# Feed-forward in chunks of 256 slots, started in the same block as attention

## The reference: one transformer block with routed experts

```
q, k, v = x @ Wq + bq, x @ Wk + bk, x @ Wv + bv       # 16 heads of 8 features
for each window of 64 tokens (starts 0, 32, ..., 192) and head:
    ow += softmax(q_w k_w^T / sqrt(8) + pos_bias) v_w
merged = ow / (number of windows that hold the token)
x = layernorm(x + merged @ Wo + bo)
vals, idx = top_k(x @ router_w.T, 2)                  # 8 experts
g = sigmoid(vals); g = g / (g.sum() + 1e-10)
for each expert e:
    h = silu(x @ w_gate[e]) * (x @ w_up[e])           # 256 hidden
    out += g_e * (h @ w_down[e])
x = layernorm(x + out)
```

## Time and profile before

| | us |
|---|---|
| median of 3 runs | 1024.05 (1019.09 to 1028.25) |
| the profiled execution | 1033.48, its span 1031.6 |
| attention up to the last context product | about 665 of the span |
| last projection to first gate product | 666.3 to 706.8 |
| chunks | 706.8 to 981.2 |
| POOL's last result DMAs | 981.2 to 992.3 |
| final block | 992.3 to 1031.6 |

### The profile page before, as it was taken

How to read it: one execution, slowest core, us unless ns; L and a number is a source line. 1 busy time by engine, 2 the same in 40 slices (tenths; PEclk the granted TensorE clock), 3 DMA queues, 4 the chain that set the end, 5 groups by cost and what they waited for, 6 DMA issues and landing times. The chain is left out here.

```text
span 1031.6 us, 32316 instructions
## 1 busy us (share of the span) xinstructions
PE 777.2 (75%) x13248; PEld 588.0 (57%) x13248; DVE 501.3 (49%) x1592; ACT 323.0 (31%) x483; POOL 442.9 (43%) x502
## 2 busy tenths in 40 slices
PE   5789789798798797887887977716887888888700
PEld 2477566475575565654755655515776667767600
DVE  7446355363453453543545544444455544554537
ACT  3134323233233232332332322204333322332218
POOL 8312533524425425234244243260555555546555
PEclk9899898898898988988989989857989889888955
DMA  6973343243233332432433220033222222221157
GB/s 179 263 218 97 95 121 100 80 129 104 67 112 103 101 94 86 128 102 65 132 95 89 85 64 22 9 112 94 83 78 78 68 67 83 81 70 57 37 213 301
DMA packets 79858, 107.33 MB, mean 104 GB/s; under 512 B 15648, under 2 KB 59296, under 8 KB 79712
## 3 DMA queue, kind: packets, MB, share of 16 engines
q1 hardware_dynamic: 70048, 85.44, 27.6%
q0 software_dynamic: 9088, 18.76, 5.4%
q10 hardware_dynamic: 576, 1.07, 0.3%
HBM read 61.05 MB, written 43.71 MB: 102 GB/s over the span
## 5 line engine op out<-in xcount | busy, mean ns | idle before, releaser
L613 DVE TENSOR_REDUCE neg_max<-score_ps 128x16 f32<-128x1024 f32 x109 | 133.5, 1225 | 262.6 <-PE score_ps L891 172.7
L1094 POOL DMA_INDIRECT results<-scaled_sb,result_at x156 | 149.9, 961 | 142.7 <-DVE scaled_sb L1165 98.9
L258 POOL DMA_INDIRECT slots<-rows_sb,slot_at x128 | 125.5, 980 | 172.9 <-DVE slot_at L730 127.7
L565 ACT ACTIVATE prob<-scoret_ps 128x1024 f32<-128x1024 f32 x112 | 114.6, 1023 | 249.9 <-PE scoret_ps L891 167.4
L944 PE MATMUL o_ps<-v_sb,prob 128*32 128x18 f32 x7168 | 108.4, 190 | 74.2 <-issue 74.2
L944 PEld LDWEIGHTS o_ps<-v_sb,prob 128*32 128x32 f32 x7168 | 88.2, 114 | 93.6 <-issue 86.9
L441 POOL TENSOR_TENSOR expo<-euler,neg_top 128x8 f32<-128x8 f32 x16 | 26.4, 1648 | 154.6 <-DVE neg_top L684 154.5
L1154 DVE TENSOR_TENSOR h_sb<-silu_sb,score_ps 128x512 f32<-128x512 f32 x39 | 26.7, 686 | 129.0 <-ACT silu_sb L1116 99.0
L928 PE MATMUL scoret_ps<-max_rows,half 128*64 128x512 bf16 x448 | 69.6, 390 | 19.2 <-DMA max_rows<-maxt_sb 15.6
L911 PE MATMUL scoret_ps<-bias_hl,fold 128*64 128x512 f16 x448 | 74.7, 416 | 0.9 <-ACT prob L565 0.4
L891 PE MATMUL scoret_ps<-blocks,stack 128*64 128x256 f16 x920 | 71.8, 278 | 0.0
(11 more groups left out here) (162 smaller groups left out, 1484.4 us busy)
## 6 DMA issues: line engine op xcount, KB each, us to landing
scratch<-qk_hl SPq DMA_DIRECT2D x128, 128.0 KB
stack<-scratch SPq DMA_DIRECT2D x32, 512.0 KB
blocks<-scratch SPq DMA_DIRECT2D x128, 128.0 KB
xin<-slots SPq DMA_DIRECT2D x39, 260.0 KB
final_y<-results SPq DMA_DIRECT2D x16, 512.0 KB, 6.9
x_sb<-in_x SPq DMA_DIRECT2D x16, 256.0 KB, 3.9
out<-y_sb SPq DMA_DIRECT2D x16, 256.0 KB, 4.7
slots<-fill SPq DMA_DIRECT2D x11, 260.0 KB
```

Source lines behind the costliest of these rows:

```text
L258: nc.gpsimd.indirect_dma_start(slots, bass.IndirectOffsetOnAxis(ap=slot_at[:, n:n + 1], axis=0), rows_sb[:, n // TT, n % TT, :], None).the ...
L565: act.activation(prob[:, (par + u) % 2, :], scoret_ps[:, :, :].rearrange("p b c -> p (b c)"), ACT.Exp).then_inc(exp_done, 1)
L613: dve.tensor_reduce(neg_max[:, par, v, :], ps[:, :, :].rearrange("p b (h k) -> p (b h) k", k=W), AX_X, ALU.max, negate=True).then_inc(max_ ...
L1094: pool.indirect_dma_start(results, bass.IndirectOffsetOnAxis(ap=result_at[s % RBUF][:, t:t + 1], axis=0), scaled_sb[:, s % RBUF, t, :], No ...
```

## The change

**Chunks.** 256 slots instead of 512, hence 71 instead of 39: 64 full and 7 spare. Each chunk has one `gate_up` of twelve matmuls of 256 slots, a `turn` of two transposes, a `down` of eight matmuls, and two indirect DMAs of 128 rows. Silu (L697) and `hidden` treat both halves of the hidden features in one instruction of 128x512.

**Weights.** Their high and low parts are made once per expert, in attention steps 4 to 11, one expert in each (`weights_high` on ACT, `weights_low` on DVE). Per chunk, ACT copies the two parts of its expert to one of three buffers (`weights_in`, L685, 128x1024).

**Table.** It is made in two pieces. The first 45 entries are made of chunks that are full after the 13th step; they are counted in step 14 (`count_known`) and written in the last step (`place_known_a`, `place_known_b`). The other 26 entries are made of pieces dealt out over chunks 13 to 21.

**No barrier.** The chunk loop stands in attention's block. `turn(0)` comes ahead of the last two contexts, `gate_up(0)` ahead of `project_out(15)`. What is left of step 15 is dealt out: PE projects after chunk 0, turns x1 after 5, makes logits after 7, ranks after 10; DVE does the residual in chunk 1, the norm in 4, and the rest in 7 to 22; POOL computes `powers(15)` after the results of chunk 4 and issues the 8 scatters of step 15 one at a time after the results of chunks 14, 16, ... 28. Spare rows are filled after load 8, expert rows after load 30. Load 45 waits for all scatters, fills and the second piece of the table.

**Scatters.** `scatter(13)` is split: four DMAs in step 14, four in the last step. `scatter(14)` runs in the last step, ahead of the first results.

**Memory.** The buffers of the chunks stand beside attention's instead of on top of them, some on `blocks` and `stack`, which are free by then.

```diff
-FULL = TOP * N_TOK // TOK
+HALF = 256
+HT = HALF // P
+FULL = TOP * N_TOK // HALF
+KNOWN = STEPS - 4
+FIRST = ((KNOWN + 1) * TOP * TOK - E * (HALF - 1) + HALF - 1) // HALF
+WBUF = 3
 # SP
+                for s in range(SLOT_CHUNKS):
+                    if s == FIRST:
+                        sp.wait_ge(filled, 16 * (SPARE + E))
+                        sp.wait_ge(scattered, 16 * TOP * TT * STEPS)
+                        sp.wait_ge(tables, 2)
+                    slots_in(s)
...
 # POOL, step and tail
+                    if last:
+                        scatter(i - 2, range(TT, TOP * TT))
+                        make_fill()
                     if not first:
                         powers(i - 1)
-                    if not first and not last:
+                    if i == STEPS - 3:
+                        table_constants()
+                    if i == STEPS - 2:
+                        scatter(i - 1, range(0, TT))
+                    elif not first:
                         scatter(i - 1)
...
-                scatter(STEPS - 2, range(0, 1))
                 deviation(STEPS - 1)
-                scatter(STEPS - 2, range(1, 4))
-                powers(STEPS - 1)
-                scatter(STEPS - 2, range(4, TOP * TT))
-                scatter(STEPS - 1)
+                for s in range(SLOT_CHUNKS):
+                    results_out(s)
+                    if s == 4:
+                        powers(STEPS - 1)
+                    if 14 <= s < 14 + 2 * TOP * TT and s % 2 == 0:
+                        scatter(STEPS - 1, range((s - 14) // 2, (s - 14) // 2 + 1))
 # ACT
+                def weights_in(s):
+                    e = table_value(act, expert_at, s, E - 1)
+                    after(act, up_ps, s + 1 - WBUF)
+                    settle(act)
+                    act.copy(w_slot[:, s % WBUF, :, :], wgu_sb[:, e, :, :]).then_inc(w_ready, 1)
...
+                for s in range(SLOT_CHUNKS):
+                    silu(s)
+                    if s + 2 < SLOT_CHUNKS:
+                        if s + 2 == FIRST:
+                            act.wait_ge(tables, 2)
+                        weights_in(s + 2)
+                        high(s + 2)
 # DVE
+                for s in range(SLOT_CHUNKS):
+                    hidden(s)
+                    if s >= LATE:
+                        scale(s - LATE)
+                    if s + 2 < SLOT_CHUNKS:
+                        low(s + 2)
 # PE
+                def gate_up(s):
+                    after(pe, h_done, s - 1)
+                    pe.wait_ge(x_low, s + 1)
+                    pe.wait_ge(w_ready, s + 1)
+                    b, w = s % HBUF, s % WBUF
+                    for n, signal in ((0, gate_ps), (1, up_ps)):
+                        for hh in range(2):
+                            cols = slice(n * HID + hh * P, n * HID + hh * P + P)
+                            out_ps = (score_ps, scoret_ps)[s % 2][:, n, hh * HALF:(hh + 1) * HALF]
+                            pe.matmul(out_ps, w_slot[:, w, 0, cols], x_lo[:, b, :], start=True, stop=False)
+                            pe.matmul(out_ps, w_slot[:, w, 1, cols], x_hi[:, b, :], start=False, stop=False)
+                            last = pe.matmul(out_ps, w_slot[:, w, 0, cols], x_hi[:, b, :], start=False, stop=True)
+                        last.then_inc(signal, 1)
...
+                for s in range(SLOT_CHUNKS):
+                    if s == FIRST:
+                        pe.wait_ge(tables, 2)
+                    e_before, e_of = e_of, table_value(pe, expert_at, s, E - 1)
+                    gate_up(s)
+                    if s == 0:
+                        project_out(STEPS - 1)
+                    if s == 5:
+                        turn_x1(STEPS - 1, 1)
...
+                    if s + 2 < SLOT_CHUNKS:
+                        turn(s + 2)
+                    if s:
+                        down(s - 1, e_before)
+                down(SLOT_CHUNKS - 1, e_of)
```

More of the change, by code:

```diff
@@ new lines, in build @@
+        qk_free = qk_f[:, :, :].rearrange("p n t -> p (n t)")
+        hl_free = qk_hl[:, :, :, :].rearrange("p n h t -> p (n h t)").bitcast(F32)
+        xt_free = xt_sb[:, 0, :]
+        region, marks, upto, number = (reuse(qk_free, early, *n) for n in ((E,), (E, PARTS), (E, E), (FIRST, E)))
+        taken, full, cum, jump, ahead, rem, rise = (reuse(qk_free, early, E) for _ in range(7))
+        first_of = reuse(qk_free, early, E + 1)
+        over, at_most, summed = (reuse(hl_free, wide, *n) for n in ((E, PARTS), (E, E), (E, E)))
@@ L748, in step, with weights_low @@
                             top_two(i - 1)
[L749 removed]
+                        if u == (6 if last else 8) and not first:
                             places(i - 1, 1 - par)
[L752 to L761 removed]
+                def weights_low(e):
+                    dve.wait_ge(w_high, e + 1)
+                    settle(dve)
+                    dve.tensor_tensor(wgu_sb[:, e, 1, :], wgu_sb[:, e, 1, :], wgu_sb[:, e, 0, :],
+                                      ALU.subtract).then_inc(w_low, 1)
                 done = [0]
@@ L804, in _ @@
+                for s in range(SLOT_CHUNKS - LATE, SLOT_CHUNKS):
+                    scale(s)
             @block.tensor
@@ L1005, in step @@
                                 bias_s(i + 2, 0)
+                        if u == NU and last:
+                            turn(0)
                         if u >= 2:
```

545 lines of the change are left out of this document (290 added, 255 removed).

## The result

The changed kernel takes **988.25 us** (median of 4 runs, 983.22 to 991.23), the kernel before 1025.09 (4 runs). The ratio is 0.964 with a 95% interval of 0.958 to 0.971. I had forecast 980, in a range of 904 to 1046. The profiled execution took 986.44, its span 984.7; my sum was 987.7 for the span.

What follows compares the result with a forecast made beforehand. The prediction took POOL's indirect DMA runs holding up PE's results to bound the chunk stage. Terms -39.8 + 7 - 17.5 + 10.4 - 4 = -43.9 gave span 987.7; plus 1.9 minus 9.4 gave 980 us, range 904 to 1046.

Steps and rivals of the forecast that it cites:

- hold: In attention and chunks: a few us into a gapless run of POOL's indirect DMAs, PE's results reach no engine until it ends.
- final block: The program's last stage, 39.3 us in the profile before: forecast unchanged, 0.
- Handover: From attention to the chunks: first gate product at 667.0 instead of 706.8, -39.8 us; bounds -41 and +3 later.
- Chunks: Chunk loop: 3.61 us per chunk of 256, times 71 = 256.3 against 273.8, so -17.5 us.
- scatter(14)'s +7: Last attention units or first chunks: its eight DMAs, now run together, cost 8.95 less 2, +7 us; bounds 0 and +9.
- The charge of 0.51 us per indirect DMA: Chunk stage: cost of the hold per POOL indirect DMA, (7.02 - 4.99) / 4; charged twice per chunk of 256.
- Step 15 inside the chunks: Chunk loop: PE 3.3, POOL 4.1 for eight more indirect DMAs, DVE 3; sum +10.4 us, bounds +4 and +16.
- End: POOL's queued results after the last chunk: 7 us instead of 11.1 before the final block, -4 us; bounds -8 and 0.
- No hold: Rival, chunks and scatters: gaps break POOL's runs, chunks take 2.59 us and the +7 goes; 897 us, chance 0.2.
- Short runs: Rival, chunk loop: runs of four DMAs with pauses of 4.24 us, 4.5 us per chunk; 1043 us, chance 0.18.
- Exposed loads: Rival, gate products: each 256-column product pays one more weight load of 0.106 us, 90 us in all; 1070 us, chance 0.05.
- It does not do what it says: Rival, handover: a queue wait keeps the first chunks back until step 15 is through, 25 of 40 us return; 1005, chance 0.1.

## Why the prediction was right, and where it was not

The times of both chips beside the terms, changed minus before, from the traces, with all four stages cut at the same events in both kernels:

| Term | forecast | first chip | chip without hold |
|---|---|---|---|
| first gate product | -39.8 | -40.4 | -40.8 |
| chunks with scatter(14) and step 15, up to the last `scale` | -17.5 + 7 + 10.4 = -0.1 | 270.47 - 274.53 = -4.1 | 197.45 - 195.52 = +1.9 |
| from there to the first load of the final block | -4 | 7.8 - 11.0 = -3.2 | 10.1 - 17.2 = -7.1 |
| final block | 0 | 40.1 - 39.3 = +0.8 | 40.2 - 39.2 = +1.0 |
| span | -43.9 | -46.9 | -45.0 |

- **Handover: right,** to 0.6 us. Nothing that `turn(0)`, the table or the weights need was late. One thing shown beside it was off: I expected PE's clock back from the 0.5 of the handover, and the first chunk's products are still 0.21 us apart, which costs about 1 us. This row is most of the change in the span, but not all of it is gain, since part of the work that stood there is paid inside the chunks. On the chips without hold the parts can be told apart by kernels, each against the kernel before on its own chip: chunks of 256 without early start are 16.7 us faster, with the early table 38.7, with step 15 dealt out 47.2. So the early start is worth some 30 of the 47 there; on the first chip these kernels did not run.
- **Chunks: right in mechanism, wrong by 4 us.** The mean of 3.75 us lies inside the 3.3 to 4.0 that I had named. It holds step 15 in it; less the 10.4 that I had put for step 15 it is 3.61, the forecast's number, but no run on the first chip shows the 10.4. What is missing is scatter(14)'s +7. It stands in the first chunks, where the fifth silu comes at 683.55 - 668.77 = 14.8 us after the first, and at 577.14 - 564.82 = 12.3 on the chip without hold: **2.5 us, not 7**. The step that failed is "a run of eight costs what its row shows": one of its DMAs went ahead alone (663.72), and the seven others ran beside the first chunks (667.90 to 676.46), which was the case of my lower bound 0. That PE's queued chunks are the reason is not shown.
- **The charge of 0.51 us per indirect DMA: about right.** The stage takes 270.5 - 197.5 = 73.0 us more on the first chip, over 142 results and 15 scatters: 0.46 each. For the kernel before it is (274.5 - 195.5) / 156 = 0.51. In attention, which I had charged only where the change touched it, 104 us over 112 scatters are 0.93 each. Part of the price is TensorE's clock: in the chunk stage it was granted 0.91 on the first chip and 0.98 on the other, and the same 1583 products kept PE busy 216.7 and 189.0 us. The clock falls behind PE's stops: from 765 to 770 PE is busy 2.1 us, and from 770 to 775 the granted clock is 0.50. So up to 28 of the 73 us are work at the lower clock, and the rest are stops of PE.
- **What I said of the hold: half right.** "A few us into a gapless run PE's results stop reaching the others until the run is over": the place and price hold, the condition doesn't. I had named runs of 6 to 8 as a sign; after the change 23 of POOL's 35 runs in the stage are of two or four DMAs, 11 of five to eight and one of ten, with 0.7 to 5.9 us between, and the hold was still there; and on the other chips runs of up to 140, in the kernel before 156, hold nothing. I had written that no row could tell whether the run was the cause or a coincidence. It costs time only together with something that the first chip had and the others had not, and I had no term for that. That the mean came out right with other runs than forecast is in part luck: the charge per DMA had been read from runs of eight.
- **Step 15 inside the chunks: the number fits, by luck.** 10.4 forecast. On the chips without hold some 10 us go there (207.5 against 196.9 us with step 15 first). But 4.1 of the forecast's 10.4 was the hold, which those chips don't have; there the 10.1 us that POOL needs for eight scatters fill the same place, a price that I had set at 4.1. On the first chip no run separates it.
- **End: right** on the first chip. I had named 7 us from the last `scale` to the first load of the final block; it is 944.62 - 937.41 = 7.2 from the end of that `scale`. No load stopped at 45 either: it was issued at 823.3, 31 us behind the last scatter of step 15.
- **The final block** is 0.8 us longer. Its first addition comes 5.8 us after the loads are issued, before 4.4 (992.34 to 996.73). Its loads now go to memory that was `blocks`. That this is the reason was not tested.
- **The median.** Forecast 980, measured 988. The sum for the span is 3 us off on the other side (987.7 against 984.7). I took 9.4 us off because the profiled run of before lay that far above its median; that of after lies 1.8 below. That step, a chance of one execution taken for a constant, is the whole of the miss, and the error of the span hides 3 us of it. Taken as a difference between like runs, -43.9 stands against a measured -36.8 in the medians and -46.9 in the spans.
- **The range** was said to take in most of the case without hold, but its lower end, 904, lies above that case's own 897, so about half of it was out.

**The rivals.** *No hold* said 897: on the first chip it is out, by a mean of 3.75 us and by the 61.9 us of waits. On chips without hold the kernel is at 811, since there attention has none either, and its 2.59 us per chunk is near what is seen there (2.54 undisturbed). *Short runs* said 4.5 us a chunk: 3.75 measured, though 12 of the 35 runs are of four and 11 of two. The pauses, 0.7 to 5.9 us, are mostly below the 4.24 that it had. *Exposed loads* is out: the twelve products of a chunk start 0.12 us apart on both chips (699.80 and 700.16 above are three products apart), each with a load of its own that is recorded with 0.19 us, where the rival asked for 0.22. By the rule of the Trainium skill, page "TensorE: Matmul & The Clock Gate", section "The mechanism", a load overlaps a running matmul only where the row group differs. The traces don't agree: these products all fill the 128 rows, and their loads overlap. *It does not do what it says* is out by the first row of the table.

**Still open.** What makes the first chip different, and whether on it the chunks with plain result DMAs would run at 2.6 us. Both theories (POOL's indirect DMAs as the other half of the cause, or any traffic of small rows) fit all that was measured there, in two kernels. PE's rows with "issue" ahead of them say only that it waits there for nothing that the profile shows. All experiments ran where there is no hold, so none of them tests its cause.

No variant beat the changed kernel with the same output. The one that did, plain result DMAs, leaves out the placing of rows; it shows that 10 to 12 us would be had if POOL's 1.26 us per 128 rows could be shared.

## What to carry to other kernels

Where a stage ends in a chain of small steps on all engines, the next stage's first items can start on what is known early: here a table of the chunks that are full three steps before the end let the first gate product start 40.4 and 40.8 us sooner on two chips that differ by a fifth in their time. Not all of that is gain: what is dealt out into the next stage is paid there, some 10 us of it here. Look for the engine whose list has no gaps, not for the one with the highest busy share: PE was busy 97% beside a POOL at 76%, and it was POOL that bound, if only by a little. Compare kernels on one chip, and spans with spans: how far one profiled run lies from its median is no constant to carry to another kernel.

## What the runs showed of the hardware

- The same program took 1025 us on one chip and 858 to 862 on four others. The difference lies almost only in stretches where GpSimd issues indirect DMAs (128 rows of 512 or 520 B) beside a busy TensorE: 0.5 us for each in the chunks, 0.9 in attention. Whether the chip or something beside it makes the difference is open.
- In these stretches, on the first chip, ScalarE started 7.6 us after the recorded end of the matmul that it waited for, where on the other chip it was 0.05, and TensorE starts one to three matmuls at a time, 0.7 or 1.4 us apart, with "issue" ahead of them. The granted clock falls to 0.50 in places and is 0.91 in the mean, against 0.98.
- An indirect DMA takes GpSimd 0.96 us and follows the last after 1.264 us, on every chip, with or without the hold.
